# Chain steps at other tiles, and a start-up that splits and spreads weights with TensorE and ScalarE

## The chip, the cores and the metric

The kernel runs on one core of one Trainium2 chip. The metric is the device time of one execution in microseconds, as the median of several; lower is better. The core has five engines that take their instructions in order and meet only at semaphores: TensorE (PE in the profile, PEld for its weight loads), VectorE (DVE), ScalarE (ACT), GpSimd (POOL) and SyncE (SP), which issues nearly all DMAs here.

## The reference

A "macaron" block on x of 16 sequences x 256 tokens x 128 features, all fp32:

```
x = x + 0.5 * ffn(layernorm(x))
x = x + attn(layernorm(x))
x = x + 0.5 * ffn(layernorm(x))
```

`ffn` is a mixture of 32 experts of width 64 with a shared expert of width 128. Router: `score = sigmoid(x @ Wr.T)`, plus a bias; of 4 groups of 8 experts the best 2 are kept (by the sum of their two best), of these the best 4 experts; their scores are normalised and scaled by 2.5. Each expert is `(silu(x Wg.T) * (x Wu.T)) Wd.T`, summed with those weights; the shared one is added unweighted. `attn` is a gated recurrence: `proj = x W_in.T`, `sigmoid(gate) * conv5(value)` per feature, a scan `h = tanh(a) * h + u` over time, then `layernorm(x + y W_out.T) * ln_w + ln_b`.

## The kernel before, in words

The 4096 tokens are cut into 8 blocks of 512. Each block goes through two FFNs (called 1 and 4 after their layer norms) with the mixer (norms 2 and 3) between them. An FFN of a block is a **unit**; `ORDER` puts the 16 units in a row: (1,0) to (1,3), then (4,0), (1,4), (4,1), (1,5), ... (1,7), and (4,4) to (4,7). I call them units 0 to 15: unit 4 is (4,0), unit 11 is (1,7), unit 15 is (4,7). Units 5, 7, 9 are of FFN 1, units 4, 6, 8, 10 of FFN 4.

A unit has 17 **tiles** j = 0 to 16: the shared expert, then 16 pairs of experts. Every tile runs:

- TensorE: gate and up products, three 128x512 matmuls each (high x high, high x low, low x high parts of the fp32 split), into `gate_ps[n % 2]` and `up_ps[n % 2]`; and three matmuls of the down product of tile j - 3 (`LAG`), the last of which reads `hid_lo`.
- ScalarE: silu of the gate bank (`silu_tile`, L581), then `hid_hi` of tile j - 1 (L589).
- VectorE: `weighted` = silu x routing weight (L728; not for tile 0), `hid` = weighted x up (L741).
- GpSimd: `hid_lo` = hid - hid_hi (L485), in two halves.

The gate matmuls of tile n wait until `weighted` of tile n - 2 has read that bank, its up matmuls for `hid` of n - 2, so VectorE and ScalarE may lag TensorE by two tiles.

Beside the tiles run the **chain steps** of other blocks: layer norms (`stats`, `meanvar` on VectorE, `norm` = four small operations on GpSimd, L493 to L499, `normalise` = four ACTIVATEs on ScalarE), transposes, the router with its 26 dependent VectorE operations (`route`, the last makes `w_tok`), the mixer. Tables by hand, read by `steps_beside`, give each step a **slot**: the tile after whose own work it is put in its engine's stream (x.5 on VectorE: behind `hid` instead of ahead of it). Middle units use the general tables, the first four `BEGIN`, the last five `END`. A step that is put ahead of what it waits for blocks its engine. All products of the chain steps on TensorE use one PSUM bank, `side`; each waits until the one before it has been read (`side_read`).

The routing weights of a unit must be spread over 128 partitions: `w_tok` is transposed into `side`, copied to `wT` by ScalarE, stored to HBM, and read back broadcast by SP in four groups of pairs (`CHUNKS` 0-2, 2-6, 6-11, 11-16), two DMAs each, into `wb`, which takes the place of the raw weights (`raw`). Weights of tile 1 and 2 are in group 0, those of tiles 3 to 6 in group 1.

**Start-up**: the weights come in 14 batches of four 128x128 tiles. TensorE transposes each into a bank (`weights`), ScalarE copies it to `wt_hi` (rounded), VectorE subtracts to `wt_lo` (L719). The routing of block 0 runs beside them on VectorE, with one `wt_lo` between every two steps:

```
for step in range(3, ROUTE):
    if step % 2 and 4 + step // 2 - 1 < NBATCH:
        weight_low(4 + step // 2 - 1)
    route_step(1, 0, first, step)
```

Behind it VectorE does `stats` and `meanvar` of block 1, whose `norm` and `normalise` follow in unit 0, slot 0.

## Time and profile before

| | |
|---|---|
| median of 3 runs | 712.45 us (711.03 to 712.47) |
| profiled execution: own time / span of its instructions | 712.7 us / 710.9 us |
| TensorE busy | 666.2 us (94%) |
| VectorE, ScalarE, GpSimd busy | 549.7 (77%), 421.3 (59%), 483.5 us (68%) |
| mean granted TensorE clock | 0.986 |
| first matmul of unit 0, of unit 15 | 28.54 us, 667.6 us |
| length of units 5, 7, 9 / 4, 6, 8, 10 | 39.7 us / 42.3 to 42.8 us |
| TensorE idle within units 0 to 15 | 3.2, 0.7, 1.8, 0.7, 1.6, 0, 1.9, 0, 1.6, 0, 1.6, 3.2, 2.0, 2.2, 6.6, 0.8 us |

The profile is of one execution. Times stand from the span's start. A bracket behind a row tells how long its engine was idle before it, and what ended that; ends of matmuls are modelled, so the distance between the starts of two rows tells more than a row's length.

### The profile page before, as it was taken

Reading aid. Unit: us, or ns where it says so; the run is one execution under the profiler, and the core shown is the slowest. Engines: PE = TensorE matmul, PEld = TensorE weight load, DVE = VectorE, ACT = ScalarE, POOL = GpSimd, SP = SyncE. Lnnn points to the kernel's source line nnn. Section 1 sums busy time; section 2 is a strip of 40 time slices with the busy share of each in tenths; the row PEclk is TensorE's granted clock in tenths of the full one; section 3 lists DMA queues with packets and bytes.
Section 4 is the critical chain, followed back from the end, with each engine's and each line's share of the span. In section 5 each row is a group of like instructions: output and inputs, shape, how many; then the busy total and the mean of one; then the engine's idle time right before and its main releaser. Section 6 shows DMA issues by size and latency. Waiting matters only on the chain. (4 is left out here: it accounts for less than half of the span.)

```text
span 710.9 us, 10396 instructions
## 1 busy us (share of the span) xinstructions
PE 666.2 (94%) x3016; PEld 530.2 (75%) x3016; DVE 549.7 (77%) x1539; ACT 421.3 (59%) x801; POOL 483.5 (68%) x717
## 2 busy tenths in 40 slices
PE   5589999999999999899999999999989989898997
PEld 5468878777877888688876888688767768776785
DVE  5778778779869798788977798788968858756765
ACT  4445666575576656666566756666565556545553
POOL 1147568686777777776876867778776776775674
PEclk9899999999999999999999999999999999999999
...
GB/s 189 107 209 43 229 4 191 80 92 165 35 207 30 164 92 114 157 27 212 18 191 79 110 133 66 201 5 190 67 75 166 4 192 62 103 138 16 108 148 16
DMA packets 60011, 78.84 MB, mean 111 GB/s; under 512 B 7697, under 2 KB 27185, under 8 KB 59953
## 3 DMA queue, kind: packets, MB, share of 16 engines
...
q14 instruction: 35, 0.28, 0.1%
...
## 5 line engine op out<-in xcount | busy, mean ns | idle before, releaser
L485 POOL TENSOR_TENSOR hid_lo<-hid,hid_hi 128x256 fp32r<-128x256 f32 x540 | 386.7, 739 | 187.3 <-ACT hid_hi L589 185.1
L728 DVE TENSOR_TENSOR weighted<-gate_ps,raw 128x512 f32<-128x512 f32 x256 | 175.0, 684 | 96.2 <-ACT gate_ps L581 85.4
L589 ACT ACTIVATE hid_hi<-hid 128x512 fp32r<-128x512 f32 x272 | 170.7, 628 | 113.7 <-DVE hid L741 111.7
L581 ACT ACTIVATE gate_ps<-gate_ps 128x512 f32<-128x512 f32 x256 | 148.6, 580 | 96.2 <-PE gate_ps L995 94.2
L741 DVE TENSOR_TENSOR hid<-weighted,up_ps 128x512 f32<-128x512 f32 x256 | 174.3, 681 | 7.3 <-DVE weighted L728 0.5
L1041 PE MATMUL down_ps<-hid_lo,wt_hi 128*128 128x512 f32 x272 | 108.5, 399 | 1.0 <-POOL hid_lo L485 0.8
L1038 PE MATMUL down_ps<-hid_hi,wt_hi 128*128 128x512 f32 x272 | 108.4, 399 | 0.0
L1039 PE MATMUL down_ps<-hid_hi,wt_lo 128*128 128x512 f32 x272 | 108.0, 397 | 0.0
L993 PE MATMUL gate_ps<-xT_hi,wt_hi 128*128 128x512 f32 x170 | 73.1, 430 | 6.4 <-DVE weighted L728 6.3
L993 PE MATMUL up_ps<-xT_hi,wt_hi 128*128 128x512 f32 x170 | 70.6, 415 | 7.2 <-DVE hid L741 7.2
L994 PE MATMUL gate_ps<-xT_lo,wt_hi 128*128 128x512 f32 x170 | 68.2, 401 | 0.0
L995 PE MATMUL gate_ps<-xT_hi,wt_lo 128*128 128x512 f32 x170 | 68.1, 401 | 0.0
L994 PE MATMUL up_ps<-xT_lo,wt_hi 128*128 128x512 f32 x170 | 68.0, 400 | 0.0
L995 PE MATMUL up_ps<-xT_hi,wt_lo 128*128 128x512 f32 x170 | 68.0, 400 | 0.0
L1041 PEld LDWEIGHTS down_ps<-hid_lo,wt_hi 128*128 128x128 f32 x272 | 51.4, 189 | 15.9 <-POOL hid_lo L485 2.8
L1039 PEld LDWEIGHTS down_ps<-hid_hi,wt_lo 128*128 128x128 f32 x272 | 51.7, 190 | 12.5
L1038 PEld LDWEIGHTS down_ps<-hid_hi,wt_hi 128*128 128x128 f32 x272 | 51.5, 189 | 12.4
L993 PEld LDWEIGHTS up_ps<-xT_hi,wt_hi 128*128 128x128 f32 x170 | 32.5, 191 | 23.0 <-DVE hid L741 16.3
L993 PE MATMUL gate_ps<-xT_hi_spare,wt_hi 128*128 128x512 f32 x102 | 43.2, 423 | 2.4 <-DVE weighted L728 2.2
L993 PEld LDWEIGHTS gate_ps<-xT_hi,wt_hi 128*128 128x128 f32 x170 | 32.8, 193 | 14.8 <-DVE weighted L728 8.8
L993 PE MATMUL up_ps<-xT_hi_spare,wt_hi 128*128 128x512 f32 x102 | 41.4, 406 | 2.0 <-DVE hid L741 2.0
L624 ACT ACTIVATE normed<-x,shift,rstd 128x128 f32<-128x128 f32 x64 | 26.4, 483 | 24.7 <-POOL shift L499 24.7
...
## 6 DMA issues: line engine op xcount, KB each, us to landing
raw<-wT_hbm SPq DMA_DIRECT2D x64, 640.0 KB, 13.6
...
```

Of the source, the lines that this page charges most:

```text
L485: last = nc.gpsimd.tensor_tensor(hid_lo[s][:, cols], hid[s][:, cols], hid_hi[s][:, cols].bitcast(F32), ALU.subtract)
L581: nc.scalar.activation(bank[:, :] if j else silu_sb[:, :], bank[:, :], ACT.Silu).then_inc(silu_done, 1)
L589: nc.scalar.activation(hid_hi[s][:, :], hid[s][:, :], ACT.Copy).then_inc(hid_hi_done, 1)
L624: last = nc.scalar.activation(normed[k][:, t, :], src[:, t, :], ACT.Identity, bias=shift[k][:, t:t + 1], scale=rstd[k][:, t:t + 1])
L728: V.tensor_tensor(weighted[j % 2][:, :], gate_ps[n % BANKS][:, :], wb[:, j - 1, :], ALU.mult)\
L741: V.tensor_tensor(hid[n % RING][:, :], factor[:, :], up_ps[n % BANKS][:, :], ALU.mult)\
L993: nc.tensor.matmul(dst, w, moving_hi, start=start, stop=False)
L994: nc.tensor.matmul(dst, w, moving_lo, start=False, stop=False)
L995: return nc.tensor.matmul(dst, w_lo, moving_hi, start=False, stop=stop)
L1038: nc.tensor.matmul(down_ps[:, :], wt_hi[:, w, :], hid_hi[s][:, :], start=(j == 0), stop=False)
L1039: nc.tensor.matmul(down_ps[:, :], wt_lo[:, w, :], hid_hi[s][:, :], start=False, stop=False)
L1041: nc.tensor.matmul(down_ps[:, :], wt_hi[:, w, :], hid_lo[s][:, :], start=False, stop=(j == NT - 1)).then_inc(down_done, 1)
```

## The change

1. **Tables.** All of `BEGIN`, `END` and the general tables get other slots. Of the general ones (FFN 4 units: `NORM4`, `PROJECT`, `ADD`, `PREPARE`; FFN 1 units: the others):

```
-        ADD = {"copy ffn 1": 2, "transpose ffn 1": 4, "add ffn 1": 4}
-        PROJECT = {"stats 2": 1, "meanvar 2": 1.5, "norm 2": 2, "normalise 2": 3, "transpose 2": 9, "xT high 2": 9,
-        NORM4 = {"meanvar 3": 0, "norm 3": 0, "normalise 3": 1, "scale 3": 2, "x2": 10, "stats 4": 12,
-                 "meanvar 4": 13, "norm 4": 14, "normalise 4": 15}
-        NEXT = {"stats 1": 12.5, "meanvar 1": 13, "norm 1": 14, "normalise 1": 15}
+        ADD = {"copy ffn 1": 1, "transpose ffn 1": 4, "add ffn 1": 8.5}
+        PROJECT = {"stats 2": 1.5, "meanvar 2": 2, "norm 2": 2, "normalise 2": 3, "transpose 2": 9, "xT high 2": 9,
+        NORM4 = {"meanvar 3": 0, "norm 3": 1, "normalise 3": 2, "scale 3": 3, "x2": 11, "stats 4": 11.5,
+                 "meanvar 4": 13, "norm 4": 14, "normalise 4": 16}
+        NEXT = {"stats 1": 13.5, "meanvar 1": 15, "norm 1": 14, "normalise 1": 16}
```

In unit 11 `transpose 2` and `xT high 2` go from slot 11 to 10 (`normalise 3` stays at 11), `mixer gate` from 14 to 11, `tanh gate` from 14 to 13; in unit 12 `x2` of block 6 goes from 13 to 12, `stats 4` from 14.5 to 13.5, `normalise 4` from 16 to 15, and `normalise 3` from 11 to 12; in unit 14 (table `REST_7`):

```
-        REST_7 = {"mixer out": 0, "mixer sum": 0, "stats 3": 0.5, "meanvar 3": 1, "norm 3": 1, "normalise 3": 2,
-                  "scale 3": 2, "x2": 3, "stats 4": 4, "meanvar 4": 4, "norm 4": 5, "normalise 4": 5, "transpose 4": 7,
-                  "xT high 4": 7, "xT low 4": 7, "router 4": 9, "silu logits 4": 10, "route 4": even(9, 13),
-                  "weights 4": 14}
+                ({"mixer out": 1, "mixer sum": 0.5, "stats 3": 0.5, "meanvar 3": 1, "norm 3": 1, "normalise 3": 2,
+                  "scale 3": 2, "x2": 3, "stats 4": 4, "meanvar 4": 4, "norm 4": 5, "normalise 4": 6,
+                  "transpose 4": 8, "xT high 4": 9, "xT low 4": 9, "router 4": 10, "silu logits 4": 11,
+                  "route 4": even(10, 14), "weights 4": 15}, 7),
```

2. **Start-up.** Fourteen transposes of the identity (`WARM`) run on TensorE before the first weights. For batches 4 to 9 (`BY_SCALAR`) the low part is no longer subtracted on VectorE: TensorE transposes the batch a second time and adds minus `wt_hi`, and ScalarE copies the result to `wt_lo`. VectorE then runs the routing steps of block 0 without a break and does batches 10 to 13 behind them. The transpose of `w_tok` stands behind batch 10, and the weights of pairs 0 and 1 of unit 0 are spread by eight 128x128 fp32 matmuls and two copies, not by a DMA.

```
+            def weights_rest(n):
...
+                pe.wait_ge(w_hi_done, n + 1)
+                for t in range(4):
+                    tile = min(4 * n + t, down_tile(0))
+                    nc.tensor.matmul(rest_bank(n)[:, t * P:(t + 1) * P], raw[:, tile, :], ident[:, :],
+                                     is_transpose=True, start=t == 0, stop=False)
+                nc.tensor.matmul(rest_bank(n), neg_ident[:, :],
+                                 wt_hi[:, 4 * n:4 * n + 4, :].rearrange("p n c -> p (n c)"), start=False, stop=True)\
+                  .then_inc(w_rest, 1)
...
+            for n in range(WARM):
+                nc.tensor.transpose(mixed[:, 0:P], ident[:, :], ident[:, :])
...
+                if n - 1 in BY_SCALAR:
+                    weights_rest(n - 1)
+                if n == ROUTED:
+                    transpose_route(1, 0)
+                if n == ROUTED + 1:
+                    pe.wait_ge(pool_const, 5 + EARLY * TT)
+                    pe.wait_ge(wT_done[1], 1)
+                    for q in range(EARLY):
+                        for t in range(TT):
+                            last = nc.tensor.matmul(early_bank[q][:, t * P:(t + 1) * P], spread[q][:, t, :], wT[1][:, :],
+                                                    start=True, stop=True)
+                        last.then_inc(early_spread, 1)
...
-                if step % 2 and 4 + step // 2 - 1 < NBATCH:
-                    weight_low(4 + step // 2 - 1)
                 route_step(1, 0, first, step)
+            for n in range(BY_SCALAR[-1] + 1, NBATCH):
+                weight_low(n)
```

ScalarE gets, in its loop over batches: `weight_low(n - 1)` behind `weight_high(n)`, `wT_copy(1, 0)` behind batch 10, the two copies of the spread weights behind batch 11. GpSimd makes eight `spread` masks of 128x128. `gdiff` and `beats` move to the PSUM bank `routed`.

Where instructions move, at the start: TensorE from batch 8's (before) or batch 9's (after) transposes to the first matmul of unit 0. `raw` are weight batches, `side<-ident,w_tok` is the transpose of the routing weights. Before:

```order
L1003 MATMUL up_ps1<-ident,raw 128x128 x4
L1003 MATMUL gate_ps0<-ident,raw 128x128 x4
L1003 MATMUL gate_ps1<-ident,raw 128x128 x3
L1006 MATMUL gate_ps1<-ident,raw 128x128
L1071 MATMUL side<-ident,w_tok 128x128
L993 MATMUL gate_ps0<-xT_hi1,wt_hi 128x512
```

and after:

```order
L1120 MATMUL gate_ps1<-ident,raw 128x128 x4
L1106 MATMUL up_ps0<-ident,raw 128x128 x4
L1108 MATMUL up_ps0<-wt_hi,neg_ident 128x512
L1185 MATMUL side<-ident,w_tok 128x128
L1120 MATMUL mixed<-ident,raw 128x128 x4
L1288 MATMUL side<-wT1,spread0 128x128 x4
L1288 MATMUL routed<-wT1,spread1 128x128 x4
L1120 MATMUL gate_ps0<-ident,raw 128x128 x4
L1120 MATMUL gate_ps1<-ident,raw 128x128 x4
L1094 MATMUL gate_ps0<-xT_hi1,wt_hi 128x512
```

The transpose of `w_tok` now has three weight batches and the eight spreading matmuls behind it and ahead of unit 0.

GpSimd in a middle unit of FFN 4, tiles 0 to 3 (`shift3` and `shift2` release the `normalise` steps on ScalarE, `scaled` is `scale 3`). Before:

```order
L499 TENSOR_TENSOR shift3<-neg_mean3,rstd3 128x4
L485 TENSOR_TENSOR hid_lo0<-hid0,hid_hi0 128x256 x2
L485 TENSOR_TENSOR hid_lo1<-hid1,hid_hi1 128x256 x2
L516 TENSOR_TENSOR scaled<-normed3,lnw_b 128x512
L493 TENSOR_TENSOR neg_mean2<-zeros,meanvar2 128x4
L495 TENSOR_TENSOR var_eps2<-meanvar2,eps 128x4
L497 TENSOR_TENSOR rstd2<-var_eps2,neg_half 128x4
L499 TENSOR_TENSOR shift2<-neg_mean2,rstd2 128x4
```

and after:

```order
L576 TENSOR_TENSOR shift3<-neg_mean3,rstd3 128x4
L562 TENSOR_TENSOR hid_lo1<-hid1,hid_hi1 128x256 x2
L570 TENSOR_TENSOR neg_mean2<-zeros,meanvar2 128x4
L572 TENSOR_TENSOR var_eps2<-meanvar2,eps 128x4
L574 TENSOR_TENSOR rstd2<-var_eps2,neg_half 128x4
L576 TENSOR_TENSOR shift2<-neg_mean2,rstd2 128x4
L562 TENSOR_TENSOR hid_lo2<-hid2,hid_hi2 128x256 x2
L593 TENSOR_TENSOR scaled<-normed3,lnw_b 128x512
```

`norm 2` has moved ahead of `scale 3`, and `norm 3` behind one `hid_lo`.

TensorE at the start of unit 14, from the last up matmul of tile 0 to the mixer's output product (`side<-wt_hi,y_hi`, 12 short matmuls). Before:

```order
L995 MATMUL up_ps0<-xT_hi4,wt_lo 128x512
L1038 MATMUL down_ps<-hid_hi3,wt_hi 128x512
L1039 MATMUL down_ps<-hid_hi3,wt_lo 128x512
L1041 MATMUL down_ps<-hid_lo3,wt_hi 128x512
L1077 MATMUL side<-wt_hi,y_hi 128x128
```

and after:

```order
L1155 MATMUL down_ps<-hid_lo3,wt_hi 128x512
L1094 MATMUL gate_ps1<-xT_hi4,wt_hi 128x512
L1095 MATMUL gate_ps1<-xT_lo4,wt_hi 128x512
L1096 MATMUL gate_ps1<-xT_hi4,wt_lo 128x512
L1094 MATMUL up_ps1<-xT_hi4,wt_hi 128x512
L1095 MATMUL up_ps1<-xT_lo4,wt_hi 128x512
L1096 MATMUL up_ps1<-xT_hi4,wt_lo 128x512
L1152 MATMUL down_ps<-hid_hi0,wt_hi 128x512
L1153 MATMUL down_ps<-hid_hi0,wt_lo 128x512
L1155 MATMUL down_ps<-hid_lo0,wt_hi 128x512
L1191 MATMUL side<-wt_hi,y_hi 128x128
```

A whole tile of nine matmuls has come ahead of the mixer's product.

## Rows read from the trace of the kernel before

**Rows 1.** Waits of TensorE from 50 us on: engine, line, releaser: us, times, longest.
```profile
PE up_ps L993 <- DVE hid L741: 9.2, 13, 3.0
PE gate_ps L993 <- DVE weighted L728: 5.4, 7, 1.0
PE side L1046 <- ACT normed L624: 4.9, 3, 2.2
```

**Rows 2.** Timeline of TensorE, start-up and unit 0: start, us, what [idle before].
```profile
16.22 1.91 PE L1003 MATMUL up_ps<-ident,raw 128*128 128x128 f32 x8
...
19.96 0.66 PE L1003 MATMUL up_ps<-ident,raw 128*128 128x128 f32 x4 [0.24 <-DMA raw<-in_L_ffn_gate_w]
...
28.45 0.45 PE L1071 MATMUL side<-ident,w_tok 128*128 128x128 f32 x1 [5.10 <-DVE w_tok L854]
...
29.12 0.63 PE L994 MATMUL gate_ps<-xT_lo,wt_hi 128*128 128x512 f32 x1
29.54 0.63 PE L995 MATMUL gate_ps<-xT_hi,wt_lo 128*128 128x512 f32 x1
...
32.90 0.40 PE L993 MATMUL gate_ps<-xT_hi,wt_hi 128*128 128x512 f32 x1
33.13 0.40 PE L994 MATMUL gate_ps<-xT_lo,wt_hi 128*128 128x512 f32 x1
...
36.31 0.50 PE L993 MATMUL gate_ps<-xT_hi,wt_hi 128*128 128x512 f32 x1 [1.42 <-DVE weighted L728]
...
43.88 0.50 PE L993 MATMUL gate_ps<-xT_hi,wt_hi 128*128 128x512 f32 x1 [1.77 <-DVE weighted L728]
```

**Rows 3.** Busy time by stretch: PE, PEld, DVE, ACT, POOL, granted clock, DMA.
```profile
45.50:48.80 3.30, 3.30 (x9) 2.65 (x8) 3.26 (x7) 1.62 (x5) 2.68 (x4) 0.50 1.07 222
```

**Rows 4.** Timeline of VectorE: the routing steps of block 0.
```profile
18.08 0.28 DVE L797 TENSOR_REDUCE best<-routed 128x16 f32<-128x128 f32 x1
18.40 0.29 DVE L799 TENSOR_TENSOR is_best<-routed,best 128x128 f32<-128x128 f32 x1
...
19.21 0.28 DVE L801 SCALAR_TENSOR_TENSOR others<-is_best,routed 128x128 f32<-128x128 f32 x1
```

**Rows 5.** Timeline of ACT: normalise of block 1, in unit 0.
```profile
31.57 1.65 ACT L624 ACTIVATE normed<-x_ln,shift,rstd 128x128 f32<-128x128 f32 x4 [0.77 <-POOL shift L499]
```

**Rows 6.** SP's broadcast DMAs and the VectorE rows that wait for them, units 0 and 15.
```profile
30.81 7.08 SPq L417 DMA_DIRECT2D raw<-wT_hbm  x8
...
35.57 0.69 DVE L728 TENSOR_TENSOR weighted<-gate_ps,raw 128x512 f32<-128x512 f32 x1 [3.34 <-DMA raw<-wT_hbm]
...
43.14 0.69 DVE L728 TENSOR_TENSOR weighted<-gate_ps,raw 128x512 f32<-128x512 f32 x1 [4.09 <-DMA raw<-wT_hbm]
...
671.32 0.69 DVE L728 TENSOR_TENSOR weighted<-gate_ps,raw 128x512 f32<-128x512 f32 x1 [1.43 <-DMA raw<-wT_hbm]
```

**Rows 7.** Timelines of POOL, ACT and PE in unit 6 (FFN 4), tiles 3 to 6.
```profile
289.29 1.31 POOL L516 TENSOR_TENSOR scaled<-normed,lnw_b 128x512 f32<-128x512 f32 x1
...
292.31 1.65 ACT L624 ACTIVATE normed<-x,shift,rstd 128x128 f32<-128x128 f32 x4 [2.65 <-POOL shift L499]
...
295.22 0.50 PE L993 MATMUL gate_ps<-xT_hi_spare,wt_hi 128*128 128x512 f32 x1 [1.01 <-DVE weighted L728]
```

**Rows 8.** Timelines of VectorE and TensorE, unit 11, tiles 11 to 13.
```profile
519.63 0.69 DVE L766 TENSOR_TENSOR xT_lo<-side,xT_hi 128x512 fp32r<-128x512 f32 x1 [2.79 <-ACT xT_hi L604]
...
521.49 0.50 PE L993 MATMUL up_ps<-xT_hi,wt_hi 128*128 128x512 f32 x1 [3.03 <-DVE hid L741]
```

**Rows 9.** Timeline of TensorE, units 13 and 14: waits for chain steps.
```profile
577.47 0.30 PE L1046 MATMUL side<-ident,normed 128*128 128x128 f32 x1 [2.22 <-ACT normed L624]
...
621.04 0.30 PE L1077 MATMUL side<-wt_hi,y_hi 128*128 128x128 f32 x1 [2.04 <-POOL y_lo L539]
...
641.97 0.30 PE L1046 MATMUL side<-ident,normed 128*128 128x128 f32 x1 [1.88 <-ACT normed L624]
...
643.08 0.79 PE L993 MATMUL gate_ps<-xT_hi,wt_hi 128*128 128x512 f32 x1 [0.49 <-DVE weighted L728]
```

More of the change, by code:

```diff
@@ L48, with lows_by_vector @@
 NBATCH = 14
+EARLY = 2
+WARM = 14
+ROUTED = 10
+BY_SCALAR = range(4, 10)
+def lows_by_vector(n):
+    return sum(i not in BY_SCALAR for i in range(n))
 def pair_tile(q):
@@ L291, in even @@
             return tuple(first + int(i * (last - first) * 2 / (n - 1) + 0.5) / 2 for i in range(n))
-        FIRST = {"norm 1": 0, "normalise 1": 0, "transpose 1": 2, "xT high 1": 2, "xT low 1": 2.5, "router 1": 4,
-                 "silu logits 1": 5, "route 1": even(4, 12), "weights 1": 13}
-        NEXT = {"stats 1": 12.5, "meanvar 1": 13, "norm 1": 14, "normalise 1": 15}
-        PREPARE = {"transpose 1": 0, "xT high 1": 0, "xT low 1": 0.5, "router 1": 2, "silu logits 1": 3,
-                   "route 1": even(2, 12), "weights 1": 13}
@@ L299, in macaron_kernel @@
-        ADD = {"copy ffn 1": 2, "transpose ffn 1": 4, "add ffn 1": 4}
-        PROJECT = {"stats 2": 1, "meanvar 2": 1.5, "norm 2": 2, "normalise 2": 3, "transpose 2": 9, "xT high 2": 9,
-                   "xT low 2": 9, "mixer gate": 11, "tanh gate": 11, "mixer value": 12, "copy value": 12,
-                   "add ln_b": 15}
-        MIXER = {"conv": (0, 0.5, 1, 2, 3, 4), "y high": 5, "y low": 5, "mixer out": 8, "mixer sum": 8,
-                 "stats 3": 14}
-        NORM4 = {"meanvar 3": 0, "norm 3": 0, "normalise 3": 1, "scale 3": 2, "x2": 10, "stats 4": 12,
-                 "meanvar 4": 13, "norm 4": 14, "normalise 4": 15}
@@ L307, in macaron_kernel @@
-        XT4 = {"transpose 4": 0, "xT high 4": 0, "xT low 4": 0.5}
-        ROUTE4 = {"router 4": 2, "silu logits 4": 3, "route 4": even(2, 12), "weights 4": 13}
-        OUTPUT = {"copy ffn 4": 2, "transpose ffn 4": 5, "halve ffn": 5, "add ffn 4": 8}
-        PROJECT_0 = {**PROJECT, "stats 2": 5, "meanvar 2": 6, "norm 2": 6, "normalise 2": 7}
-        TAPS = {"conv": (14, 14.5, 15, 15.5, None, None)}
-        MIXER_0 = {**MIXER, "conv": (None, None, None, None, 0, 0.5), "y high": 1, "y low": 1, "mixer out": 5,
-                   "mixer sum": 5, "stats 3": 6}
@@ new lines, in macaron_kernel @@
+        PROJECT = {"stats 2": 1.5, "meanvar 2": 2, "norm 2": 2, "normalise 2": 3, "transpose 2": 9, "xT high 2": 9,
+                   "xT low 2": 9.5, "mixer gate": 10, "tanh gate": 10, "mixer value": 12, "copy value": 12,
+                   "add ln_b": 16}
+        NORM4 = {"meanvar 3": 0, "norm 3": 1, "normalise 3": 2, "scale 3": 3, "x2": 11, "stats 4": 11.5,
+                 "meanvar 4": 13, "norm 4": 14, "normalise 4": 16}
+        PREPARE = {"transpose 1": 0, "xT high 1": 1, "xT low 1": 1, "router 1": 2, "silu logits 1": 3,
+                   "route 1": even(2, 12), "weights 1": 13}
```

190 lines of the change are left out of this document (141 added, 49 removed), and 8 rows, old and new, of the table END.

## The prediction

> **What bounds the kernel now.** I read the table of busy times first: TensorE is busy 94% of the span, every other engine under 78%. So the time is TensorE's matmuls plus its idle time plus what its clock costs. Next the waits of TensorE [rows 1]: it waits mostly for VectorE's `hid` (9.2 us) and `weighted` (5.4 us) and for ScalarE's `normed` (4.9 us), in 23 pieces. The table of idle time per unit tells where: units 5, 7, 9 have none (39.7 us each, what the matmuls take), units 4, 6, 8, 10 have 1.6 to 1.9, unit 11 has 3.2, unit 13 2.2, unit 14 6.6. Then the timelines around each of these. In all 27.9 us of idle time lie within the units, and 28.5 us pass before the first. The reader is to see that each long wait is one chain step that sits ahead of a tile's work in an in-order engine; the tile's work pays.
>
> The clock adds to it. Two 128x512 matmuls start 0.42 us apart at 29.1 us (1.2 GHz) and 0.23 us apart at 32.9 us (2.4 GHz) [rows 2]. After the waits of 1.77 us (unit 0), 2.22 (unit 13), 2.04 and 1.88 (unit 14) [rows 2, 9] TensorE ran 3.3 us at a granted clock of 0.50 [rows 3], shown for the first of them. Such a stretch costs 3.3 x (1 - 0.23/0.42) = 1.5 us. The wait of 3.03 us in unit 11 [rows 8] was followed by none, so this price is likely, not sure.
>
> **The start-up.** Routing steps on VectorE: two steps next to each other start 0.32 us apart (18.08, 18.40), with a `wt_lo` between them 0.81 (18.40, 19.21) [rows 4], so each subtraction costs the chain 0.49. Ten of them go: 4.9 us. The transpose of `w_tok`, now at 28.45 after a wait of 5.10 us [rows 2], can run at about 23.5, if TensorE is there by then. It has more to do: a batch of four transposes starts over 0.9 us at the low clock (eight in 1.91) and takes under 0.66 at the high one [rows 2]; six extra batches and six 128x512 matmuls are 6 x (0.5 + 0.23) = 4.4 us at the high clock, 6 x (0.9 + 0.42) = 7.9 at the low. Batch 4 begins two batches ahead of the row at 16.22, at 14.5; seven batches plus the extra take 7.9 us at the high clock, 14.2 at the low. With the rise near 18 us as now: 14.5 + 3.5 + (14.2 - 3.5)/1.8 = 23.9. So 23.5 to 24.
>
> What comes behind it eats the gain. The copy of `wT` ends at 24.2. The spreading matmuls (128x128, true fp32) have no row; bounds from near ones are 0.11 (a transpose, half of 0.23) and 0.42 us each, I take 0.23: 8 x 0.23 = 1.9 us (0.9 to 3.4). By the Trainium skill, FP8 and Floating Point Precision, section TensorE Precision Notes, true fp32 takes four passes, for which a quarter of a 512-column row each would again be 0.23, an estimate; no row here shows it. Then two copies of 0.5, batches 12 and 13 (transpose, high, low): about 2.4 us. VectorE ends its last subtraction at 28.5 (27.5 to 30), and unit 0 starts when it started before. The warm-up transposes lie in the time in which TensorE waits for the first weights anyway (5.1 us).
>
> **Unit 0.** Before, its fourth tile's gate waited for `weighted` of tile 1 until 36.31 [rows 2], because group 0 of the broadcast landed at 35.5 [rows 6]. Now that group is on the chip by 27. Next late is block 1's `normalise`, which stands ahead of tile 1's silu on ScalarE: 31.57 to 33.2 before [rows 5], 31.9 to 33.5 now, as VectorE's `stats` start 0.3 later; silu 0.5, `weighted` 0.7: the fourth gate at 34.9. Gain 1.4. Group 1: SP's first broadcast starts at 30.81 now, groups 0 and 1 take until 43.1 [rows 6], that is 4.8 and 7.5 us. After, the store starts at 24.2 and the broadcast at 25.8, group 1 lands at 33.3 to 35.5; tile 3 wants it at 36. So the wait of 1.77 us and the low clock behind it (1.5 us) go. Together 4.7 us; if the new idle time (some 1.7 us at 33) costs a low stretch, 3.2. I take 4.0.
>
> **Units 4, 6, 8, 10.** GpSimd did `scale 3` (1.31 us) ahead of `norm 2`; ScalarE stood 2.65 us before `normalise 2`, silu of tile 4 came behind it, VectorE's `weighted` at 294.5, and TensorE waited 1.01 us, then 0.4 for `hid` and 0.2 for `hid_lo` [rows 7]. After, `norm 2` comes first. It then waits for `meanvar 2`, which stands behind the first routing step and so behind the router's product, at about 287; `shift2` at 289, `normalise 2` until 290.7, `weighted` of tile 4 done by 292, and gate 6 wants it at 294.2: no wait, 2 us spare. `scale 3` delays one `hid_lo` that has 1.5 us to spare. Gain 1.6 a unit, less what is new: 6.2 (4 to 6.6). The router's and mixer's other steps move with the same check: `add ffn 1` at 8.5 is done 1.2 us before `transpose 2` wants `side`; `xT low 2` 0.6 us before `mixer gate`.
>
> **Units 1 to 3** have 3.1 us of idle time in five pieces; half goes, I take 1.5 (0 to 2.5).
>
> **Units 11 to 13.** In 11, VectorE stood 2.79 us for `xT high 2`, which ScalarE had behind `normalise 3`; TensorE lost 3.03 [rows 8]. With it one slot earlier the wait shrinks to the delay of silu 12, 0.7 us; but `tanh gate` at 13 now holds `side` when `weights 4` wants it, 0.7 more: gain 1.6 (1 to 2.6). Unit 12: 0.5 (0 to 1.5), from `normalise 4` of block 5. Unit 13's 2.22 us [rows 9] was `normalise 4` of block 6, one tile (2.1 us) too late; it is one tile earlier now, and 1.5 us of clock go with it, but `scale 3` and `x2` back to back on GpSimd (2 x 1.3) make a `hid_lo` late by 0.75: gain 2.9 (1.5 to 3.7).
>
> **Unit 14.** The mixer's product waited 2.04, the transpose 1.88, a gate behind it 0.49 [rows 9]; each moves back a tile of 2.1 us, so these go, with two low stretches: 4.4 + 3.0. New: `mixer sum` at 0.5 blocks VectorE from tile 0's `hid` until the product at the end of tile 1; `sum` 0.7, `stats` 0.9, `meanvar` 0.4 and then `weighted` and `hid` of tile 1 come 0.8 us late. Gain 6.6 (4 to 8.5). `weights 4` comes a tile later too, and unit 15's first two `weighted` already waited for the broadcast [rows 6] (1.43 us for the first): group 0 now lands 5.7 us into the unit, and gate 3 wants its product at 6.3: cost 0.3 (0 to 1).
>
> **New tight places.** `norm 1` sits at slot 14 on GpSimd and waits for `meanvar 1` at VectorE's slot 15; `hid_lo` of tile 14 is done at about the moment its down matmul wants it, in seven units: 1.0 us (0 to 3).
>
> **Sum.** 4.0 + 1.5 + 6.2 + 1.6 + 0.5 + 2.9 + 6.6 - 0.3 - 1.0 = 22.0. The profiled execution took 712.7 us (710.9 span and 1.8 around it): 690.7. Its median sibling is 0.25 us lower: 690.5.
>
> **Rivals.**
> - *Slots give back half.* Each table entry was only walked along its own chain; tiles where two moved steps meet (12.5 to 13 in FFN 1 units, unit 2's `xT high 2` at 11) may turn into waits of 0.5 to 1 us. For it: ScalarE and GpSimd already waited longest on each other. Against: the spare times above. Of the chains' 18.0 us (22.0 less unit 0) half stay: 699.5.
> - *Everything goes.* All upper ends: 4.7 + 2.5 + 6.6 + 2.6 + 1.5 + 3.7 + 8.5 = 30.1, 682.4.
> - *The clock stays low through the start-up.* Then batch 4 to the transpose of `w_tok` takes 14.2 us, until 28.7; spreading and batches 12 and 13 at the low clock add 2: unit 0 starts 6 us later, 696.5. Transposes at 16.2 us run at the low clock, at 19.9 at the high one [rows 2], after nothing but transposes since 13.6: they do raise it, so little is left for this. The Trainium skill, TensorE: Matmul & The Clock Gate, Part 4: PE-mode transpose, says transposes do not count as busy for the clock; by that rule this rival is what happens, and the trace speaks against it.
> - *Slower.* GpSimd's wait for `meanvar 1` is long, not even: if `hid_lo` of tile 14 comes 2.0 us late in the seven units, TensorE idles 2.0 and each time loses 1.5 to the clock: 24.5 us in place of the 1.0 above, 714.0. It decides from 1.8 us on. Against: VectorE is two tiles ahead of what the down product needs.
>
> **How the numbers follow.** Forecast 0.60 (686 to 696), half given back 0.18 (696 to 705), everything 0.10 (681 to 686), low clock 0.07 (694 to 699), slower 0.04, no change 0.01. For 8 in 10 the range goes from 684 to 701. Under 0.2% (1.4 us) cannot be told from no change. Faster 0.95, same 0.01, slower 0.04.
>
> **What would show it.** Right: the transpose of `w_tok` at 23.5 to 24; first gate at 28 to 29; no VectorE wait for a broadcast in unit 0; fourth gate near 35; units 4, 6, 8, 10 at 40.7 to 41.2 us with idle time under 0.3; unit 14 at about 44; at most two low stretches behind unit 0. Wrong: units 5, 7, 9 over 40 us (new waits), TensorE at 0.42 us a row past 20 us, or unit 0's start past 30.

## The result and the profile after

| | before | after |
|---|---|---|
| median, in the same session | 711.74 us (710.66 to 712.47) | 681.43 us (680.44 to 682.35) |
| ratio, 95% interval | | 0.9575 (0.9551 to 0.9599) |
| span of the profiled execution | 710.9 us | 678.4 us |
| TensorE busy | 666.2 us | 659.7 us |
| unit 0 begins | 28.54 us | 28.40 us |
| idle within the units, TensorE | 27.9 us in 36 waits | 9.1 us in 17 waits |

The kernel gained 30.3 us, the forecast was 22.0 and the time lies 2.6 us below the range. By unit (length, start to start of their first gate products; in brackets the idle time of TensorE behind that start, and the number of waits, those under 0.15 us included, which the view of waits leaves out):

| | before | after | gained | forecast |
|---|---|---|---|---|
| start and unit 0 | 28.54 + 42.37 (3.19, 2) | 28.40 + 37.26 (1.15, 2) | 5.25 | 4.0 |
| 1 to 3 | 125.31 (3.09, 6) | 120.75 (0, 0) | 4.56 | 1.5 |
| 4, 6, 8, 10 | 170.09 (6.74, 13) | 159.69 (0, 0) | 10.40 | 6.2 |
| 5, 7, 9 | 118.96 (0, 0) | 118.39 (0, 0) | 0.57 | -1.0 |
| 11 | 45.51 (3.23, 2) | 42.88 (1.19, 2) | 2.63 | 1.6 |
| 12 | 42.17 (2.03, 3) | 40.71 (1.00, 2) | 1.46 | 0.5 |
| 13 | 43.80 (2.22, 1) | 40.25 (0.09, 1) | 3.55 | 2.9 |
| 14 | 50.85 (6.64, 7) | 45.81 (4.17, 7) | 5.04 | 6.6 |
| 15 | 43.30 (0.77, 2) | 44.25 (1.55, 3) | -0.95 | -0.3 |

The waits of TensorE from 50 us on, after, against [rows 1] (engine, line, releaser: us, times, longest):

```profile
PE down_ps L1152 <- ACT ffn_sb L681: 2.1, 1, 2.1
PE side L1185 <- DVE w_tok L953: 1.8, 2, 1.0
PE side L1094 <- DVE xT_lo L865: 0.9, 1, 0.9
PE up_ps L1094 <- DVE hid L840: 0.9, 2, 0.5
```

The 13 waits for `hid` have become two, the three for `normed` none, the seven for `weighted` one of 0.2. The largest is a new one, for `ffn_sb`.

The timeline of TensorE after, in the start-up and unit 0, against [rows 2]:

```profile
8.42 0.66 PE L1160 MATMUL side<-ident,normed 128*128 128x128 f32 x4 [1.70 <-ACT normed L712]
...
16.56 0.78 PE L1108 MATMUL up_ps<-wt_hi,neg_ident 128*128 128x512 f32 x1
...
18.02 0.48 PE L1108 MATMUL down_ps<-wt_hi,neg_ident 128*128 128x512 f32 x1
...
22.77 0.30 PE L1185 MATMUL side<-ident,w_tok 128*128 128x128 f32 x1
...
23.88 1.13 PE L1288 MATMUL side<-wT,spread 128*128 128x128 f32 x8 [0.38 <-ACT wT L704]
24.85 1.06 PE L1288 MATMUL routed<-wT,spread 128*128 128x128 f32 x8
...
28.40 0.50 PE L1094 MATMUL gate_ps<-xT_hi,wt_hi 128*128 128x512 f32 x1 [1.62 <-DVE wt_lo L814]
28.74 0.40 PE L1095 MATMUL gate_ps<-xT_lo,wt_hi 128*128 128x512 f32 x1
28.97 0.39 PE L1096 MATMUL gate_ps<-xT_hi,wt_lo 128*128 128x512 f32 x1
...
33.52 0.63 PE L1160 MATMUL side<-ident,normed 128*128 128x128 f32 x4 [0.66 <-ACT normed L712]
34.64 0.50 PE L1094 MATMUL gate_ps<-xT_hi,wt_hi 128*128 128x512 f32 x1 [0.49 <-DVE weighted L827]
```

The transpose of `w_tok` is at 22.8 (forecast 23.5 to 24), the first gate at 28.4 behind VectorE's last `wt_lo` (28 to 29), the fourth gate at 34.6 (34.9). Four fp32 matmuls (a group of eight records) start over 0.97 us, 0.24 each (forecast 0.23). Unit 0 starts at once at 0.23 us a row; before, it ran at 0.42 until 31.7.

The stretch of [rows 3], after (columns: busy PE, PEld, DVE, ACT, POOL, granted clock, DMA share):

```profile
45.50:48.80 3.30, 3.30 (x16) 2.66 (x15) 3.17 (x10) 2.28 (x4) 2.08 (x4) 1.00 0.01 2
```

Sixteen rows in place of nine. Before, five such stretches of 0.43 us a row (29.1 to 31.7, 45.5 to 48.9, 578.4 to 581.3, 623.0 to 625.6, 643.7 to 646.2) had 14.1 us, which took 14.1 x (1 - 0.233/0.427) = 6.4 us more than at the high pace; after, there is none past 17.3 us. The first of the five cost less than its share, as told below.

The routing steps on VectorE after, against [rows 4], and ScalarE's `normalise` of block 1, against [rows 5]:

```profile
16.18 0.29 DVE L896 TENSOR_REDUCE best<-routed 128x16 f32<-128x128 f32 x1
16.50 0.29 DVE L898 TENSOR_TENSOR is_best<-routed,best 128x128 f32<-128x128 f32 x1
16.83 0.29 DVE L900 SCALAR_TENSOR_TENSOR others<-is_best,routed 128x128 f32<-128x128 f32 x1
```

```profile
31.73 1.65 ACT L712 ACTIVATE normed<-x_ln,shift,rstd 128x128 f32<-128x128 f32 x4 [1.72 <-POOL shift L576]
```

The steps stand 0.32 apart without a subtraction between them, and `normalise` starts where the forecast had it (31.9).

VectorE in unit 15 after, against the last row of [rows 6]:

```profile
639.37 0.69 DVE L827 TENSOR_TENSOR weighted<-gate_ps,raw 128x512 f32<-128x512 f32 x1 [2.94 <-DMA raw<-wT_hbm]
```

It waits twice as long as before, but TensorE, which it may lag by two tiles, pays nothing for this: its wait there (0.78 us) is for `ffn_sb`.

GpSimd in unit 6 after, against [rows 7]: the step `norm 2` (rows from 275.81) now ahead of `scaled`:

```profile
275.81 0.20 POOL L570 TENSOR_TENSOR neg_mean<-zeros,meanvar 128x4 f32<-128x4 f32 x1
...
277.32 0.20 POOL L576 TENSOR_TENSOR shift<-neg_mean,rstd 128x4 f32<-128x4 f32 x1
277.47 1.43 POOL L562 TENSOR_TENSOR hid_lo<-hid,hid_hi 128x256 fp32r<-128x256 f32 x2
278.87 1.29 POOL L593 TENSOR_TENSOR scaled<-normed,lnw_b 128x512 f32<-128x512 f32 x1
```

TensorE in unit 11, against [rows 8], waits 0.90 us in place of 3.03:

```profile
494.79 0.47 PE L1094 MATMUL side<-xT_hi,wt_hi 128*128 128x512 f32 x1 [0.90 <-DVE xT_lo L865]
```

and in unit 14, against [rows 9], the product and the transpose follow the row before them without a wait, and a down product waits instead:

```profile
592.69 0.40 PE L1155 MATMUL down_ps<-hid_lo,wt_hi 128*128 128x512 f32 x1
592.93 0.22 PE L1191 MATMUL side<-wt_hi,y_hi 128*128 128x128 f32 x1
...
601.95 0.50 PE L1152 MATMUL down_ps<-hid_hi,wt_hi 128*128 128x512 f32 x1 [2.08 <-ACT ffn_sb L681]
...
612.05 0.39 PE L1155 MATMUL down_ps<-hid_lo,wt_hi 128*128 128x512 f32 x1
612.28 0.60 PE L1160 MATMUL side<-ident,normed 128*128 128x128 f32 x4
```

### The profile page after: what moved, and what is told of

The parts are those of the page before. It is cut to its first block and busy times, and to the rows that moved or that the text cites. A ratio compares the mean times of both kernels' runs of the same rounds, so it can differ in the third digit from the quotient of the medians.

```text
span 678.4 us, 10540 instructions
## 1 busy us (share of the span) xinstructions
PE 659.7 (97%) x3076; PEld 532.5 (78%) x3076; DVE 546.8 (81%) x1534; ACT 423.2 (62%) x809; POOL 485.4 (72%) x725
## 5 line engine op out<-in xcount | busy, mean ns | idle before, releaser
L1094 PE MATMUL gate_ps<-xT_hi,wt_hi 128*128 128x512 f32 x170 | 71.5, 421 | 2.5 <-DVE wt_lo L814 1.6
L1094 PE MATMUL up_ps<-xT_hi,wt_hi 128*128 128x512 f32 x170 | 68.1, 401 | 0.9 <-DVE hid L840 0.9
L1094 PEld LDWEIGHTS up_ps<-xT_hi,wt_hi 128*128 128x128 f32 x170 | 31.9, 188 | 11.8 <-DVE hid L840 4.6
L1096 PE MATMUL gate_ps<-xT_hi_spare,wt_lo 128*128 128x512 f32 x102 | 40.3, 395 | 0.0
L1096 PE MATMUL up_ps<-xT_hi_spare,wt_lo 128*128 128x512 f32 x102 | 40.3, 395 | 0.0
## 6 DMA issues: line engine op xcount, KB each, us to landing
raw<-wT_hbm SPq DMA_DIRECT2D x64, 640.0 KB, 13.5
```

The costliest lines, as they stand in the source:

```text
L1094: nc.tensor.matmul(dst, w, moving_hi, start=start, stop=False)
L1096: return nc.tensor.matmul(dst, w_lo, moving_hi, start=False, stop=stop)
```

## The experiments

The first eight ask which part of the change gave what; the others ask what a wait costs and whether the waits left can go.

**The two halves.** e1_tables is the kernel before with all the new tables, e2_startup the changed kernel with all the old ones.

```
 e1   (kernel before)   BEGIN, END, ADD, PROJECT, NORM4, ... = those of the changed kernel
 e2   (changed kernel)  BEGIN, END, ADD, PROJECT, NORM4, ... = those of before
```

> The kernel before with all the new tables and its old start-up. Theory A (two separate parts): the tables give what units 1 to 15 lost between the two traces, 27.2 us, and the start-up 5.3, so about 684.5 us. Rival B (the start-up also sets how units 1 to 3 run, since their broadcasts and norms hang on it): units 1 to 3 keep their waits, 689 to 690 us. My prediction's own terms for the chains would give 694.5 us.

Measured: 687.66 us (686.55 to 689.2) against 712.35, ratio 0.9666 (0.9639 to 0.9694): 24.7 us, 3.2 less than theory A had. Rival B is out: units 1 to 3 took 120.7 us without a wait, as in the changed kernel. What theory A missed lies in units 11, 12, 14 and 15, which are 0.5, 0.5, 1.1 and 2.2 us longer than in the changed kernel.

> The changed kernel with all the old tables. Theory A: 5 us faster than before, about 707 us, unit 0 shorter by 5 and all other units as before with their waits. Rival B: 702 us or less, because the earlier start removes waits in units 1 to 3 too. Rival C (the start-up's gain came from the new slots of unit 0): no more than 2 us faster, 710 us.

Measured: 708.29 us (704.5 to 709.32), ratio 0.993 (0.9907 to 0.9954): 4.1 us, nearer to theory A than to rivals B and C. Its ten executions fall into two groups (704.5 to 705.8 at a mean granted clock of 0.988 to 0.993, 708.2 to 709.3 at 0.981 to 0.983), so this figure holds to some 2 us only; the profiled one is of the second group. The two add up to 28.8 of the 30.3, and the 1.5 us between lie within the two intervals. The tables gave the bulk and most of the surplus (24.7 where the forecast had 18.0 for the chains); the start-up gave about what was forecast.

**One slot.** e3_scale3 changes one number of the kernel before, e8_two that and one other, e4_middle all tables of units 4 to 10.

```
 e3, e8  -  "scale 3": 2      (NORM4)     e8 only  -  "add ffn 1": 4    (ADD)
         +  "scale 3": 3                           +  "add ffn 1": 8.5
 e4      +  NORM4, PROJECT, ADD, PREPARE, MIXER, ROUTE4, OUTPUT, NEXT of the changed kernel, units 4 to 10 alone
```

> The kernel before with one number changed: scale 3 at slot 3 instead of 2 in the general table, so that norm 2 comes ahead of it on GpSimd in units 4, 6, 8 and 10. If a wait of TensorE costs its idle time as the profile gives it, the four units lose 6.7 us: 705 us. If a wait costs the whole distance between starts, 0.2 to 0.3 us a wait more: 9 us, 702.5 us. If the two-tile slack that I worked out is wrong, the waits stay and the time is 709 to 712 us.

> The kernel before with two numbers changed for units 4, 6, 8, 10: scale 3 at slot 3, and add ffn 1 at 8.5 instead of 4, which stood ahead of tile 4's hid on VectorE. If these two steps are all that made TensorE wait there, the four units come to 40.0 us each with no idle time, like with all the new slots: 2.4 us less each than before, 702 us. If one wait is only replaced by the next, they stay at 41 us or more. Each wait removed beyond the idle time should give 0.25 us (before: three waits, 1.62 us idle, 42.3 us; with scale 3 alone two waits, 0.66 us idle, 41.1 us).

> The kernel before with the new general tables in units 4 to 10 alone. Idle-time price: 6.7 us, 705 us. Price by distances between starts: 11 us, 700.8 us, with units 4, 6, 8, 10 at 39.9 us and 5, 7, 9 at 39.5 us. Rival: the new slots need new ones in the neighbouring units too, and waits come up at the seams (units 4 and 11): 703 us or more.

| | median (range), ratio and interval | units 4, 6, 8, 10 each | idle in each (waits) |
|---|---|---|---|
| before | 712.3 | 42.34 to 42.81 | 1.62 to 1.86 (3 to 4) |
| e3 | 706.74 (704.79 to 709.84), 0.9934 (0.9903 to 0.9966) | 41.10 to 41.53 | 0.65 to 0.84 (2 to 3) |
| e8 | 703.15 (702.72 to 705.5), 0.9883 (0.9858 to 0.9909) | 40.61 to 41.08 | 0.22 to 0.45 (1 to 2) |
| e4 | 699.36 (699.26 to 700.92), 0.9834 (0.9811 to 0.9858) | 39.99 to 40.03 | 0 |

The row of the forecast was right on the mechanism: moving `scale 3` behind `norm 2` takes the long wait away. But in e3 a second step is then late, `add ffn 1`, put ahead of `hid` of tile 4 on VectorE: TensorE waits 0.42 for `hid`. e8 moves that one too and comes to 40.6 to 41.1, neither the 40.0 of its theory nor the 41 of its rival: a wait of 0.22 for `weighted` is left. So the tables had to be moved together, and e4 shows no wait in units 4 to 10. The length falls faster than the idle time: from three waits to none the idle time falls by 1.62 and the unit by 2.35 us, 0.24 more for each wait.

**The start-up's parts.** Each is the changed kernel with one part undone.

```
 e5_nowarm   -WARM = 14      +WARM = 0
 e6_noearly  -EARLY = 2      +EARLY = 0          (weights of pairs 0 and 1 by DMA again)
             -side_read = (early_copied, 1)      +side_read = (wT_done[1], 1)
 e7_sbuf     gdiff and beats in SBUF again, not in the PSUM bank `routed`
```

> The changed kernel without the 14 transposes of the identity. If they only raise the clock for the transposes of block 0's norm at 8.4 us, the routing of block 0 and unit 0 come 0.4 to 0.5 us later: 682 us. If they also keep the clock up in the weight batches, unit 0 starts up to 6 us later: 687 us. If transposes don't count for the clock, nothing changes: 681.4 us.

Measured: 683.53 us (681.58 to 683.82), ratio 0.9593 (0.9565 to 0.9621), the interval overlaps the changed kernel's. The transpose of `w_tok` came at 23.27, 0.50 later, as the first of the three cases has it, but unit 0 begins at 28.58, 0.18 later, which is less than that start varies between runs of one code (below). So the warm-up transposes bought nothing that can be told here; the other 2.7 us of the profiled span (681.3) lie in units 4 and 10, in stretches told of below. The transposes of `normed` at 8.5 took 1.12 us against 0.66, but TensorE then waited for `xT_lo` and was slow from 10.6 (here 11.1) to about 17 in both.

> The changed kernel with EARLY = 0: no spreading by TensorE, group 0 comes by broadcast in unit 0 too. Theory: group 0 lands at about 30 us, and tile 1's silu, held up by block 1's normalise, comes at 33, so the spreading bought nothing for tiles 1 and 2; unit 0 starts about 1.5 us earlier, but group 1 lands 4.8 us later, at 37.5, when tile 3 wants it: 680 to 681 us. Rival (my prediction's reading that the 4.8 us are gained in full): 2 to 4 us slower, 684 to 685 us, with VectorE waiting for group 1.

Measured: 680.63 us (679.44 to 681.43), ratio 0.9559 (0.9537 to 0.9581): not slower without the eight matmuls and two copies. TensorE and VectorE of e6_noearly, around the start of unit 0 and the fourth gate:

```profile
26.05 0.50 PE L1094 MATMUL gate_ps<-xT_hi,wt_hi 128*128 128x512 f32 x1 [1.57 <-DVE wt_lo L814]
...
32.55 0.50 PE L1094 MATMUL gate_ps<-xT_hi,wt_hi 128*128 128x512 f32 x1 [0.77 <-DVE weighted L827]
```

```profile
31.81 0.69 DVE L827 TENSOR_TENSOR weighted<-gate_ps,raw 128x512 f32<-128x512 f32 x1 [3.06 <-DMA raw<-wT_hbm]
```

Unit 0 begins 2.35 us earlier (28.40 to 26.05). VectorE waits for the broadcast again, but it lands at 31.7, and silu of tile 1 could not start before 30.9 behind `normalise` of block 1: TensorE pays 0.77 in place of 0.49. What brought group 0 forward was the earlier `w_tok`, not the spreading on TensorE. The two medians alone don't tell (the intervals overlap), but the traces do: unit 0 ends at 63.7 to 64.4 us in the five without the spreading (e6, e11, e12, e13, e15) and at 65.5 to 66.6 in the seven with it (the changed kernel, e2, e5, e7, e9, e10, e14). That part costs more than it saves.

> The changed kernel with gdiff and beats back in SBUF. I had given this move no time. Units 11 and 12 wait 1.19 and 1.00 us in the changed kernel and 1.72 and 1.50 us with the new tables on the old start-up, which also has these two in SBUF: if the move is the cause, this run shows the latter two, and units 4, 6, 8, 10 at 40.0 instead of 39.9 us, in all 1.4 us more, 682.8 us. If not, the lengths are those of the changed kernel.

Measured: 684.45 us (683.76 to 685.11), ratio 0.9614 (0.9592 to 0.9636): 3.0 us slower where 1.4 was expected; its interval and the changed kernel's just overlap. The profile sorts this. Of its 4.5 us of span, 0.7 is the start (29.13, which also varied by as much between runs of one code, below), 1.3 a stretch in unit 8 (told of below), and 1.1 a stretch in unit 14, where the granted clock is 0.53 for 3.2 us behind the same wait of 2.07 us; e14_price, which has the two in PSUM, has that stretch too (unit 14 at 46.91). What is left, 1.4 us, is near what was expected and where: unit 12 waits 1.51 for `w_tok` in place of 0.98 (0.5 longer, as in e1_tables: 41.2 in both), units 4, 6 and 10 are 0.1 longer; unit 2 has a wait of 0.33 for `hid_lo` (0.5 longer), which e1_tables had not, and unit 11 kept its length against the expectation. So the move is worth something near 1 us, not 3. The steps `gdiff` and `beats` themselves take 0.22 us in SBUF and 0.23 in PSUM; a mechanism (GpSimd against VectorE in SBUF would be one) was not shown.

**What a wait costs.** e14_price puts waits alone into the changed kernel.

```
                     up_tiles(k, m, j)
+                    if (k, m) == (1, 4) or ((k, m) == (1, 5) and j % 2):
+                        pe.wait_ge(silu_done, first_tile(k, m) + j + 1)
```

> The changed kernel with short waits put into units that have none: in unit 5 TensorE waits for ScalarE's silu of each tile before its down products (17 tiles), in unit 7 at every second tile (8), in unit 9 nothing. The silu ends about 1.5 us after the tile's gate product starts, the up product is issued by 1.4, so each wait should show some 0.1 to 0.3 us of idle time. Nothing is left out of the computation. Theory (a wait costs its idle time and about 0.25 us more): with 17 waits of 0.2, unit 5 grows by 17 x 0.45 = 7.6 us from 39.46, unit 7 by 3.6, while the idle time grows by 3.4 and 1.6. Rival (the loss is what the idle time says, and the 0.25 of the other runs came from something else that the tables moved): the two lengths grow by the idle time alone, 3.4 and 1.6.

Measured: 688.62 us (688.04 to 690.49), ratio 0.9684 (0.9655 to 0.9713). Unit 5 went from 39.46 to 44.37 (+4.91) with 17 waits, unit 7 to 41.53 (+2.07) with 8, unit 9 stayed at 39.47. TensorE's waits in unit 5 as the profile of e14_price shows them:

```profile
PE down_ps L1152 <- ACT gate_ps L669: 0.5, 1, 0.5
PE down_ps L1152 <- ACT silu_sb L669: 0.4, 1, 0.4
```

Two waits, 0.94 us in all. The other fifteen show no idle time, because the row before is drawn 0.40 long and ends later than the next begins. The timeline of TensorE around one of them:

```profile
251.04 0.40 PE L1095 MATMUL up_ps<-xT_lo,wt_hi 128*128 128x512 f32 x1
251.27 0.40 PE L1096 MATMUL up_ps<-xT_hi,wt_lo 128*128 128x512 f32 x1
251.64 0.50 PE L1152 MATMUL down_ps<-hid_hi,wt_hi 128*128 128x512 f32 x1
251.97 0.40 PE L1153 MATMUL down_ps<-hid_hi,wt_lo 128*128 128x512 f32 x1
252.21 0.40 PE L1155 MATMUL down_ps<-hid_lo,wt_hi 128*128 128x512 f32 x1
```

From start to start, 0.37 and 0.33 in place of 0.23 twice: 0.24 us lost and no bracket. Beyond the idle time shown, unit 5 lost (4.91 - 0.94)/17 = 0.23 a wait, unit 7 (2.07 - 0.24)/8 = 0.23. The theory stands, its idle times did not (0.06 a wait, not 0.2). The rival is out: it allows 0.94 us.

The weight loads (PEld) do show these waits. In unit 5, and around the same row:

```profile
PEld down_ps L1152 <- ACT gate_ps L669: 6.7, 15, 0.9
```

```profile
251.63 0.19 PEld L1152 LDWEIGHTS down_ps<-hid_hi,wt_hi 128*128 128x128 f32 x1 [0.41 <-ACT gate_ps L669]
```

The silu ends at 251.58. The load behind it starts together with its own matmul, where a load in the stream starts with the matmul before (251.98 and 251.97), 0.23 ahead of its own; the row is then 0.50 long in place of 0.40, which is the 0.10 between 0.33 and 0.23. So the 0.24 of a wait without a bracket is all that it costs; in the two with one (0.42 and 0.51) the same distances give 0.27 beyond it. The Trainium skill, TensorE: Matmul & The Clock Gate, Part 2: What happens when you issue a matmul, says that a matmul in a stream hides its drain under the fill of the next and an isolated one can't; by its formulas for one bf16 matmul alone and for the gap in a stream that is (398 + 512)/2.4 less 512/2.4 + 2.5, in ns, so 0.16 us, an estimate. The runs show 0.23.

**The waits that are left.** e9_copy moves one step of unit 14 that stood behind the largest new wait.

```
-                    normalise 3, then copy ffn 4 (ScalarE's unit loop)
+                    copy ffn 4, then normalise 3
-                ({"copy ffn 4": 3, "transpose ffn 4": 4, ...}, 5),
+                ({"copy ffn 4": 2, "transpose ffn 4": 4, ...}, 5),
```

> The changed kernel with one edit: in unit 14 ScalarE does `copy ffn 4` of block 5 at slot 2 and ahead of `normalise 3`, not at slot 3 behind it. In the changed kernel the copy ran at 601.33 and TensorE's first down product of the unit waited 2.08 us for it. Theory (the step moved behind a long in-order block is what costs): the copy now runs at about 598.1, in the time in which ScalarE waits for GpSimd's `shift` anyway; TensorE then waits only for `weighted` of tile 3 (done at 601.6, wanted at 601.3): unit 14 goes from 45.8 to 44.0 us, the whole to 679.6 against the changed kernel's 681.4. Rival (silu of tile 3 behind `normalise 3` sets the place anyway): the wait turns into one for `weighted`, unit 14 stays over 45.3, the whole within 0.5 of 681.4.

Measured: 681.06 us (680.43 to 682.04), ratio 0.9566 (0.9542 to 0.959); unit 14 at 45.89. The theory fell; the rival's numbers hold (over 45.3, within 0.5), its cause does not. The wait of 2.08 went, and TensorE and VectorE of e9_copy show what took its place:

```profile
605.31 0.40 PE L1096 MATMUL gate_ps<-xT_hi,wt_lo 128*128 128x512 f32 x1
607.29 0.50 PE L1094 MATMUL up_ps<-xT_hi,wt_hi 128*128 128x512 f32 x1 [1.58 <-DVE hid L840]
```

```profile
605.37 0.87 DVE L853 BATCH_NORM_STATS2 stats<-x 128x6 f32<-128x128 f32 x4 [1.48 <-POOL x L601]
...
606.58 0.66 DVE L840 TENSOR_TENSOR hid<-weighted,up_ps 128x512 f32<-128x512 f32 x1
```

`stats 4` stands ahead of `hid` of tile 4 and waits for `x2`, which the copy had covered. The next step in the chain was late by nearly as much.

e10_ends takes, on top of e9's edit, every wait of the last five units, e11_both adds e6's edit, e12_routed11 puts the transpose of `w_tok` behind batch 11.

```
 e10  unit 11  xT low 2: 11 -> 10.5, tanh gate: 13 -> 12;  unit 12  weights 4: 12 -> 13
      unit 14  norm 4: 5 -> 4, normalise 4: 6 -> 5, transpose 4: 8 -> 7, xT high/low 4: 9 -> 8, router 4: 10 -> 9,
               silu logits 4: 11 -> 10, route 4: even(10, 14) -> even(9, 14), add ffn 4: 4 -> 6
      unit 15  transpose ffn 4: 2 -> 3
 e11  EARLY = 0          e12  EARLY = 0, ROUTED = 11
```

> e9's edit and the other waits that the changed kernel's last five units still show, each by one slot: unit 11 `xT low 2` 11 to 10.5 and `tanh gate` 13 to 12 (waits of 0.90 and 0.29); unit 12 `weights 4` 12 to 13 (0.98); unit 14 `norm 4` 5 to 4, `normalise 4` 6 to 5, `transpose 4` 8 to 7, `xT` high and low 9 to 8, router 10 to 9, `silu logits` 11 to 10, the routing steps spread from 9 to 14 in place of 10 to 14, `add ffn 4` of block 5 from 4 to 6 (waits of 0.19, 0.49, 0.38, 0.84); unit 15 `transpose ffn 4` 2 to 3 (0.78). Theory (a wait costs its idle time and about 0.25 us more): unit 11 -0.9, unit 12 -1.2, unit 14 -4.5, unit 15 -1.0: 673.8. Rival 1 (a wait costs its idle time alone): the same waits give 6.5 us, 674.9. Rival 2 (VectorE is the bound at the end of unit 14: its 26 routing steps and 17 tiles leave it no spare time once TensorE no longer stops): waits for `hid` grow back there, unit 14 stays over 43.5, 676.5 or more.

Measured: 679.61 us (678.92 to 680.81), ratio 0.9546 (0.9521 to 0.9571): 1.8 us and not 7.6. Unit 11 gave 1.1, unit 14 1.1, unit 15 0.2; unit 12 got `normed` (0.77) in place of `w_tok` (0.98), unit 13 lost 0.7, unit 14 a wait of 1.55 for `hid`. Rival 2's numbers hold (unit 14 at 44.7, the whole over 676.5), and its mechanism in part: late in unit 14 three waits for `hid` of 1.0 us in all stay in e10 to e13 and in e15. There VectorE (third column behind the length) is busy 9.57 of 10 us in e15:

```profile
617.00:627.00 10.00, 8.90 (x36) 6.08 (x35) 9.57 (x38) 4.11 (x9) 5.48 (x8) 1.00 0.00 1
```

The wait of 1.55 and those of units 12 and 13 neither rival names: they came from steps put ahead of a tile.

> e10's tables with the weights of pairs 0 and 1 not spread by TensorE but read back by DMA as in the kernel before (as in e6_noearly, which took 680.63 against the changed kernel's 681.43). Theory: unit 0 starts 2.35 us earlier and is 0.85 longer, and the gain of 0.8 to 1.5 adds to e10's: 672.6. Rival (e6's difference was scatter between runs, the two intervals overlap): within 0.4 of e10.

Measured: 678.56 us (677.38 to 680.97), ratio 0.9523 (0.9499 to 0.9548). Not the theory's 672.6, which rested on e10's, but 1.05 less than e10. Its profiled execution had a wait of 1.72 us for a broadcast in unit 15 and a low stretch behind it, which e12, with the same code there, had not.

> e11 with the transpose of w_tok behind weight batch 11 in place of 10. In e6_noearly TensorE waited 0.50 us for w_tok with batches 11 to 13 still to do, and VectorE then 0.97 us for the next rounded batch. Theory: batch 11 fills that wait, unit 0 starts 0.5 us earlier, the transpose is no later; group 0 of the broadcast lands as before: 0.5 less than e11. Rival: the fourth gate waits for the broadcast and block 1's normalise and not for the start, so unit 0 gets longer by what it starts earlier: within 0.3 of e11.

Measured: 677.83 us (677.16 to 679.13), ratio 0.9522 (0.9496 to 0.9547); unit 0 begins at 25.87. The differences from e10 to e11 to e12 have the expected sign but each is within the scatter.

e13_slots puts the steps that e10's trace showed ahead of a tile's work behind it, and e15_best takes one of its moves back.

```
 e13  unit 11  meanvar 4: 15 -> 14.5, norm 4: 15 -> 14, normalise 4: 16 -> 15;  unit 12  normalise 4: 15 -> 16
      unit 14  stats 4, meanvar 4: 4 -> 4.5, normalise 4: 5 -> 6, transpose 4: 7 -> 8, xT low 4: 8 -> 8.5
 e15  unit 11  normalise 4: 15 -> 16
```

> e12_routed11 with the steps that e10's trace shows in front of a tile's work put behind it: unit 14 `stats 4` and `meanvar 4` from 4 to 4.5 (VectorE stood 1.45 us for `x2` ahead of `hid` of tile 4, TensorE lost 1.55), `normalise 4` from 5 to 6, `transpose 4` 7 to 8, `xT low 4` 8 to 8.5; unit 11 `meanvar 4` 15 to 14.5, `norm 4` 15 to 14, `normalise 4` 16 to 15 (wait of 0.77 for it at the start of unit 12); unit 12 `normalise 4` from 15 to 16, behind silu of tile 16 (wait of 0.49 in unit 13). Theory (the waits of e10 came from these steps and have spare time behind them): unit 12 -1.0, unit 13 -0.7, unit 14 -1.8 to -2.5: 3.5 to 4 us less than e12's 677.8, 674.1. Rival (as in e9, the chain itself is what is late, and a step put behind a tile's work makes the next step's wait longer by as much): within 1 us of e12.

Measured: 677.96 us (676.61 to 680.06), ratio 0.9542 (0.9517 to 0.9567). Unit 13 -0.8 and unit 14 -0.95 as the theory has it, but unit 12 +1.7. TensorE's waits in unit 12:

```profile
PE side L1178 <- DVE xT_lo_spare L865: 1.1, 1, 1.1
PE gate_ps L1094 <- DVE weighted L827: 1.0, 1, 1.0
```

> e13_slots with `normalise 4` of block 5 in unit 11 back from slot 15 to 16, behind silu of tile 16; its `meanvar 4` and `norm 4` stay earlier. In e13_slots that `normalise 4` held silu of tile 16 for GpSimd's `shift`, VectorE's `weighted` stood 3.96 us and TensorE lost 1.02 and 1.07 at the start of unit 12. Theory (the step is right only where its input is there before the tile's work is): both waits go, and the 0.77 of e10_ends too, since `shift` now comes 1.4 us earlier; unit 12 at 40.0 in place of 42.5, the whole 2 to 2.5 us less than e13's 678.0: 675.7. Rival (the start of unit 12 is bound by the chain of block 5 whichever way it is put): unit 12 stays over 40.7, 677.5.

Measured: 675.61 us (675.17 to 677.02) against 713.04, ratio 0.9484 (0.9461 to 0.9508). Unit 12 at 39.96. The theory holds: the waits of unit 12 were those of one step's place, not of the chain's length. This version beats both kernels; its waits from 50 us on:

```profile
PE up_ps L1094 <- DVE hid L840: 0.9, 2, 0.6
PE gate_ps L1094 <- DVE weighted L827: 0.7, 1, 0.7
PE side L1302 <- ACT ffn_sb L805: 0.6, 1, 0.6
PE down_ps L1155 <- POOL hid_lo L562: 0.6, 2, 0.4
```

## Why the prediction was wrong

The direction and nearly every place were right; the size was short by 10.5 us of span (32.5 against 22.0). The largest single part is the price of a wait: 36 have become 17, and 19 x 0.23 is 4.4 us.

- **Units 4, 6, 8, 10: "Gain 1.6 a unit".** This is the step that failed. I took a wait's idle time as its price. The units had 13 waits and have none: 6.74 us of idle time and 13 x 0.23 = 3.0 us that no bracket shows (e14_price), together 9.7 of the 10.4 measured. [rows 7] held it: the gate at 295.22 is drawn 0.50 long and not 0.40. The mechanism was right, shown by e3, e8 and e4: `normalise 2` no longer stands before the tiles, and the spare time was enough.
- **Units 1 to 3, "half goes".** All went: 3.1 us of idle time and six waits, 4.5 of the 4.6 measured. Halving for prudence was unfounded: the same moves were in these tables.
- **New tight places, -1.0.** None came. `hid_lo` of tile 14 did not make TensorE wait in any of the seven middle units, and units 5, 7, 9 became 0.2 us shorter each. So the slower rival, which hung on this place, is out as well. The prediction took their 39.7 us for what the matmuls take; each held two waits for `hid` that only the weight loads show (0.7 us there in each, starts 0.29 and 0.30 apart in place of 0.23 in unit 5), and they are gone.
- **Start-up and unit 0, 4.0.** Measured 5.25 of span, e2 alone 4.1 of time. Times and durations held within 1 us. The unhedged sum was 4.7. I took 4.0 for a low stretch that might have followed the new idle time at 33, and none did. The fourth gate came at 34.64, 0.26 earlier than forecast, and the wait that went cost about 0.27 more than its 1.77 and its low stretch. That TensorE is now at the high clock from the start of unit 0 (before, low at 29.1 to 31.7) gave next to nothing: the fourth gate waits for `weighted` of tile 1 either way. The reason given for the fourth gate was half right: not the spreading but the earlier `w_tok` did it (e6). The low-clock rival is out: from 17.3 us on the rows stand at the high pace.
- **Units 11, 12, 13.** 1.6, 0.5 and 2.9 forecast, 2.6, 1.5 and 3.55 measured; each at its place. Their idle time fell by 2.0, 1.0 and 2.1 us, and the low stretch in 13 took 1.4 more; some 0.6 us of unit 11 lies in waits that only the weight loads show (there five for `hid` before, two of them with a bracket, and one after). Of unit 12's gain some 0.5 is not the tables': with `gdiff` and `beats` in SBUF it has a wait of 1.51 in place of 0.98 (e7, e1).
- **`gdiff` and `beats` in PSUM, no term.** The prediction put nothing for this move. It is worth about 1 us, in units 12, 4, 6, 10 and perhaps 2 (e7); why is open.
- **Unit 14, 6.6.** Measured 5.0. The two waits and two low stretches went, but a 2.08 wait came: `copy ffn 4` of block 5 at slot 3 stands behind `normalise 3`, which waits for a chain that `mixer sum` now starts a tile later. I followed the chain and VectorE but not what stands behind `normalise 3` on ScalarE. e9 shows that the copy alone is not the price: behind it `stats 4` is late by 1.5 us. That no low stretch followed the 2.08 wait in this execution is luck in part: one did in e1, e7 and e14.
- **Unit 15, -0.3.** Measured -0.95, by `ffn_sb`, not by the broadcast.
- Of the rivals, "everything goes" (682.4) was nearest, and right for the wrong reason: not every wait went (9.1 us are left), each was worth more.
